# The turn of the next queries moved behind the scores of 384 keys

## What is computed

```python
xn = _layernorm(x, axis=-1)
x = x + attn(xn, ...) + ffn(xn, ...)
# attn, B = 8, S = 512, NH = 16, NOPE = 128, ROPE = 64, VD = 128, QR = 128, KVR = 64
norm_q = rmsnorm(x @ W_cq, q_scale)
q_nope = (norm_q @ W_dq_nope).reshape(B, S, NH, NOPE)
q_rope = (norm_q @ W_dq_rope).reshape(B, S, NH, ROPE)
norm_kv = rmsnorm(x @ W_ckv, kv_scale)
k_nope = (norm_kv @ W_dk_nope).reshape(B, S, NH, NOPE)
value = (norm_kv @ W_dv).reshape(B, S, NH, VD)
k_rope = (x @ W_krope).reshape(B, S, 1, ROPE)
q_rope = apply_rope_single(q_rope, cos, sin)
k_rope = apply_rope_single(k_rope, cos, sin) / NH
query = jnp.concatenate([q_nope, q_rope], axis=-1)
key = jnp.concatenate([k_nope, jnp.broadcast_to(k_rope, k_nope.shape[:-1] + (ROPE,))], axis=-1)
scores = jnp.einsum('bhqd,bhkd->bhqk', query, key) * scale
scores = jnp.where(causal[None, None, :, :], scores, -1000000000.0)
attn = jax.nn.softmax(scores, axis=-1)
out = jnp.einsum('bhqk,bhkd->bhqd', attn, value)
return out.transpose(0, 2, 1, 3).reshape(B, S, NH * VD) @ W_o
```

## Time and profile before

| | |
|---|---|
| median of 3 runs | 1854.5 us (1851.81 to 1855.62) |
| profiled execution: its own time | 1855.27 us |
| profiled execution: span from the first to the last instruction | 1853.5 us |
| mean granted TensorE clock, share of full speed | 0.895 |
| TensorE / VectorE / ScalarE / GpSimd busy | 79% / 60% / 50% / 31% |

### The profile page before, as it was taken

One profiled execution on the slowest core, in us unless ns is written; L12 is line 12 of the kernel. 1 busy time (PEld: TensorE's weight loads), 2 busy tenths in 40 slices (PEclk: granted clock), 3 DMA queues, 4 the chain that ended last, 5 costly groups with the idle time before them and its releaser, 6 DMA issues. The chain is left out here.

```text
span 1853.5 us, 37109 instructions
## 1 busy us (share of the span) xinstructions
PE 1467.5 (79%) x10112; PEld 1248.0 (67%) x10113; DVE 1115.1 (60%) x4335; ACT 930.9 (50%) x2739; POOL 569.7 (31%) x640
## 2 busy tenths in 40 slices
PE   2663499989899999999999986799998888885340
PEld 2552378868688777878878764588887777774330
DVE  2896276656566676766666644555555666664464
ACT  1330276656566666666666644366665555552000
POOL 1120043433343343433433430000001433335565
PEclk8676699999999999999999997799999998998665
DMA  3993611321411111111111107654545665665553
GB/s 143 329 375 123 232 56 56 113 88 47 147 58 60 49 52 60 58 62 58 58 54 47 50 21 239 201 163 157 159 153 163 197 184 183 193 194 179 148 168 112
DMA packets 169539, 240.29 MB, mean 130 GB/s; under 512 B 16786, under 2 KB 142738, under 8 KB 165010
## 3 DMA queue, kind: packets, MB, share of 16 engines
q1 hardware_dynamic: 146322, 183.61, 29.9%
q0 software_dynamic: 18432, 50.36, 8.8%
q10 hardware_dynamic: 4608, 4.20, 0.8%
HBM read 115.42 MB, written 122.68 MB: 128 GB/s over the span
## 5 line engine op out<-in xcount | busy, mean ns | idle before, releaser
L988 ACT ACTIVATE prob<-prob,negmax 128x512 f32<-128x512 f32 (+3 forms) x512 | 285.3, 559 | 302.1 <-DVE negmax L1066 300.8
L1066 DVE CUSTOM_DVE_ANT_0 prob<-ps,mask_add 128x512 f32<-128x512 f32 (+3 forms) x512 | 244.2, 485 | 147.4 <-issue 144.2
L61 PE MATMUL ps<-kt_hi,qt_hi 128*128 (+4 forms) x512 | 188.5, 368 | 21.7 <-issue 18.7
L816 POOL DMA_INDIRECT sorted_x<-xn_row,row_no x192 | 188.3, 981 | 49.4 <-issue 45.0
L826 POOL TENSOR_TENSOR spread<-rinv,one 128x512 f32<-128x512 f32 x64 | 66.6, 1040 | 380.0 <-DVE rinv L1072 380.0
L63 PE MATMUL ps<-kt_hi,qt_lo 128*128 (+4 forms) x512 | 166.4, 325 | 0.0
L62 PE MATMUL ps<-kt_lo,qt_hi 128*128 (+4 forms) x512 | 166.0, 324 | 0.0
L910 PE MATMUL ps<-ident,prob 128*128 128x128 f32 x1280 | 160.6, 273 | 0.0
L926 PE MATMUL ps<-pt,nkv 128*64 128x512 f32 (+3 forms) x1024 | 152.0, 439 | 2.3 <-DVE lat L1084 2.3
L910 PEld LDWEIGHTS ps<-ident,prob 128*128 128x128 f32 x1280 | 143.5, 140 | 0.2 <-ACT prob L988 0.2
L1001 ACT ACTIVATE pt<-ps 128x1024 f32<-128x1024 f32 (+2 forms) x130 | 130.4, 1003 | 19.8 <-PE ps L910 16.9
(11 more groups left out here) (240 smaller groups left out, 4481.4 us busy)
## 6 DMA issues: line engine op xcount, KB each, us to landing
sorted_x<-zeros SPq DMA_DIRECT2D x16, 2048.0 KB, 9.4
rows_in<-sorted_x SPq DMA_DIRECT2D x128, 256.0 KB, 2.8
sorted_y<-rows_out SPq DMA_DIRECT2D x128, 256.0 KB
nqt<-nqt_dram SPq DMA_DIRECT2D x16, 512.0 KB
raw_gu<-in_wgu SPq DMA_DIRECT2D x16, 384.0 KB, 4.0
x_in<-in_x SPq DMA_DIRECT2D x8, 512.0 KB, 4.2
xn_dram<-xn SPq DMA_DIRECT2D x8, 512.0 KB, 5.0
xnt_dram<-xnt_hi SPq DMA_DIRECT2D x16, 256.0 KB, 4.7
```

Source lines behind the costliest of these rows:

```text
L61: pe.matmul(out, lh, rh, start=first, stop=False, **kw)
L816: pool.indirect_dma_start(sorted_x, bass.IndirectOffsetOnAxis(ap=row_no[par][:, k:k + 1], axis=0), xn_row[par][:], None).then_inc(scattere ...
L988: act.activation(prob[:, i, qt, 0:w], prob[:, i, qt, 0:w], ACT.Exp, bias=negmax[:, i, qt:qt + 1], scale=-1.0, accum_out=rowsum[:, g // 2 % ...
L1066: dve.tensor_tensor_reduce(prob[:, i, qt, 0:w], s_ps[k % 2][:, 0:w], mask[:, S - w:S], -1.0, -MASKED, ALU.add, ALU.min, negmax[:, i, qt:qt ...
```

## The change

In odd steps two groups of calls swap places. On TensorE `queries_turn` goes from before `scores(.., 1)`, the 384 keys, to behind it, so it stands right before `values`. On ScalarE the two `queries_hi` go from before the exponentials of 512 keys to behind those of 384 keys. VectorE, GpSimd and SyncE have the same instructions in the same order as before, and no instruction is added or taken away.

```diff
@@ TensorE's step @@
                 if par == 0 and bt.next_pair(p):
                     queries(*bt.next_pair(p), 4 * todo[0] + 2 * todo[1] + todo[2] + 1 if todo else None)
+                if g < NH:
+                    scores(bt.now, g, 1)
                 if par == 1 and bt.next_pair(p):
                     queries_turn(*bt.next_pair(p))
-                if g < NH:
-                    scores(bt.now, g, 1)
                 if par == 1 and bt.back(g, 3):
                     b, h = bt.back(g, 3)
                     values(b, h // 2)
@@ ScalarE's step @@
-                if nxt and par == 1:
-                    queries_hi(*nxt, 0)
-                    queries_hi(*nxt, 1)
                 if g < NH:
                     exps(bt.now, g, 0)
                 if nxt and par == 0:
                     queries_latent(*nxt)
                 if g < NH:
                     exps(bt.now, g, 1)
+                if nxt and par == 1:
+                    queries_hi(*nxt, 0)
+                    queries_hi(*nxt, 1)
                 if par == 1 and bt.back(g, 5):
```

## The result

The changed kernel takes **1916.65 us** (median of 4 runs, 1910.52 to 1921.39) against 1853.15 us (4 runs, 1850.81 to 1855.62) for the kernel before on the same chip: ratio 1.0341, interval 1.0306 to 1.0375. The forecast was slower by 50.7 us, with a range of 1899 to 1914. It became slower by 63.5 us, and the median lies 2.65 us above the range.

What follows compares the result with a forecast made beforehand. The prediction took TensorE to bound the heads stage. 62 steady steps by 0.83 us (51.5), plus 0.8 for the first odd step, minus 1.6 at round ends, gave +50.7 on 1854.5: 1905 us, range 1899 to 1914.

Steps and rivals of the forecast that it cites:

- TensorE's step price: Each of 62 steady odd steps gets 0.83 us longer on TensorE, 51.5 us in all.
- The size of that wait: In each odd step the 384-key scores wait about 1.3 us for `negmax`, in sum near 83 us.
- ScalarE's and VectorE's side at nothing: Later high and low parts and maximum of 256 keys delay nobody; costed at nothing, with 3 us kept for the range.
- The first odd step: The first odd step, without value products or copy ahead of the maximum, costs 0.8 us more (0 to 1).
- the term of the round ends: Two loop rounds ending with a fill wait up to 0.83 us less each; -1.6 us taken (0 to -1.7).
- The range: Whole kernel: 1899 to 1914 us for 8 in 10, the likeliest case's range and the near end of slower rivals.
- likeliest case: Whole kernel slower by the odd steps' price, spanning 1900 to 1912 us with its own bounds; 82%.
- The clock rival: TensorE's clock falls behind the new waits, at most 1.7 us each: 1915 to 1925, 8%; at every step 2010, 1%.
- The rival of a slipping turn: On TensorE the turn slips past the waiting 384-key scores; step length unchanged, sum near 0; no chance given.
- a stall given back: The added stall is regained in the same pair through a second TensorE wait of 0.8 us; no change, 2%.
- The fall that the forecast worked out: By the transpose rule, a wait next to 18 transposes drops TensorE's clock nearly always: the 2010 case, 1%.

Runs made afterwards that it cites:

- e2: Changed kernel with VectorE's last maximum of each even step ahead of the copy of `pt`; 1874.17 us, 1.0091 against the kernel before.
- e3: Changed kernel with the last maximum of each even step ahead of VectorE's rope sum; 1852.86 us, 0.9986 against the kernel before.
- e9: Kernel before with TensorE's part of the change and the even step's last maximum ahead of the rope sum, ScalarE as before; 1844.03 against 1858.1 us, 0.9934.
- e4: Kernel before with ScalarE's part of the change alone, TensorE's order as before; 1865.13 us, 1.0055 against the kernel before.
- e12: Kernel before with 120 extra transposes (240 instructions) ahead of TensorE's first queries; 1865.55 us, 1.0040 against the kernel before.
- e6: Kernel before with the changed order in step g = 7 alone, the last of each round; 1797.92 us, 1.0073 against the kernel before.
- e7: Kernel before with TensorE's part of the change alone, ScalarE as before; 1843.61 against 1783.56 us, 1.0332.
- e11: Changed kernel with 32 extra transposes (64 instructions, results unused) ahead of TensorE's first queries; 1908.08 against 1858.1 us for the kernel before, 1.0262.
- e10: Kernel before with the last maximum of each even step ahead of the rope sum, TensorE and ScalarE as before; 1867.25 us, 1.0040.

## Why the prediction was right and where it failed

- **TensorE's step price** ("The step is 0.83 us longer"): right. Measured 0.81 to 0.82 in each of 62 steps, 50.5 of the 51.5 us. The mechanism, the hidden wait of line 880 for the last maximum of the even step, was read from the wait condition and a gap of 0.16 us in the earlier trace rows, and e2, e3 and e9 show it: each place that this maximum moves forward takes away its part of the wait.
- **The size of that wait**: forecast 1.3 each, near 83 in sum; measured 1.23, 76.5. The matrix work's start followed the read-out by 0.06 and not by 0.16, as the 0.16 was set by the turn that still ran. Against it the turn and the change to the value products took 1.60 and not 1.53, so that the step came out at 0.81 all the same. That the two misses cancel is luck.
- **ScalarE's and VectorE's side at nothing**: right in sum. The maximum of 256 keys was "just met" (0.15 idle ahead of it), and no wait for `qt_lo` or `lat_lo` appeared. e4 shows that this rests on TensorE being late itself: alone, ScalarE's part costs 10 us, where at most 3 stood in the range.
- **The first odd step**: 0.8 forecast, 1.15 measured.
- **The step that failed is the term of the round ends**, "against it stands a gift": -1.6 forecast, +11.3 measured. The forecast looked at the two round ends with a fill and took the other four at nothing. Even of those two only one got shorter (6.28 to 5.68), and the other longer (6.32 to 7.51).
- **The range**: with the forecast's own bounds the upper end of its likeliest case is 1854.5 + 53.3 + 1 + 3 + 2 = 1914, not 1912. No bound covered a round end that grows.
- **The clock rival** was put in the wrong place. It priced a fall behind the new wait in the steps, and no step shows one: between the round ends the granted clock stayed at 1.00 with 62 waits of 1.23 us. The falls came behind the round ends, the longer ones above all, and go with the 6.0 us of slower work in the sum. Its price of at most 1.7 us was also too low: 7 us at a granted 0.57 lose 3.0. The windows that it was read from lie behind a round end too.
- **The rival of a slipping turn, and of a stall given back**: neither happened. The weight load of the turn starts at 946.19, behind that of the scores ahead of it and 0.18 ahead of its own matmul. The Trainium skill, "TensorE: Matmul & The Clock Gate", section "Architectural detail", has the queue pull weight loads ahead of matmuls that run; here the load did not pass a matmul that waits. The fall that the forecast worked out from the Trainium skill, "TensorE: Matmul & The Clock Gate", section "Part 4: PE-mode transpose", does not come: 946 to 950 holds turn and transposes among other matmuls, next to a wait of 1.25 us, at a granted clock of 1.00. No run here has transposes alone.

**What stays open.** Why TensorE asks for the first piece of code later in the new order was not shown: no view gives the moment at which it reads the end of a piece. That e12 changed nothing, and that within one kernel single round ends fall on the other side (3.89 at the last one of e9, 1.93 at the fourth of e6), says that order and cut are two conditions of several. At nine ends, and in the whole round behind each, no piece of code is recorded, and whether it was not moved or not recorded isn't known. The two large data queues have the same number of packets in all 14 profiles (146322 and 18432), which speaks for pieces that were not moved. It is not settled either why the clock stayed full behind a wait of 2.17 and fell behind one of 1.83.

## What to carry to other kernels

Before a wait is traded away, read the wait conditions of the instruction that comes in its place, in the code: a wait that ends while something else runs is in no list of waits, but the distance between its releaser's end and its start (here 0.16 us) gives it away. The order pays only if what frees the buffer is made first: with the maximum ahead of the sum, TensorE's part of the move went from 3.3% slower (e7) to 0.7% faster (e9). And a loop's round end is not a constant to add: if a wait moves close to it, count on it to change by 1 to 4 us each, clock included, and put that in the range.

## What the runs showed of the hardware

- Over the 47 round ends with recorded pieces and no fill, TensorE restarted 4.40 us or more after the first of two 16 KB pieces of code and 2.66 us or more after the second. Where the first was late that is 3.25 to 3.89 us of idle time, elsewhere 1.70 to 2.32.
- 64 unused instructions ahead of the loop (e11) took the six round ends from 25.5 to 19.1 us of wait; 240 in the kernel before (e12) changed nothing there.
- 62 waits of 1.23 us, one per 12.8 to 15.6 us, left the granted clock at 1.00. One of 3.25 us left 0.57 over the next 7 us.
- Over the 7 us behind a restart, the 15 late round ends have a granted clock of 0.57 to 0.77. Of the 32 early ones, with waits of 1.70 to 2.32 us, 18 have 0.76 or 0.77 and 14 have 1.00.
- A maximum of 128 keys put ahead of VectorE's sum delayed the sum, and the turn that reads it, by 0.10 us (e10), where 0.28 was expected.
